# A graph attention layer and a routed feed-forward layer on one core: plain 128-row loads, node sums split between two engines, weight splits moved, the adjacency stream started later

## What is computed

```python
h = inlayer2 @ W.T + b
f1, f2 = h @ w1 + b1, h @ w2 + b2
logits = f1[:, None] + f2[None, :]
bias = -1e9 * (1 - (adj > 0))
x = x + softmax(leaky_relu(logits, 0.01) + bias) @ layernorm(x)
xf = layernorm(x)
probs = softmax(xf @ gate_w + gate_b)          # top 2 of 8 kept: cw
for each expert e:
    acc += cw[:, e] * (gelu(xf @ W1[e] + b1[e]) @ W2[e] + b2[e])
out = x + acc
```

## Time and profile before

| | before |
|---|---|
| median of 3 runs | 521.45 us (521.21 to 522.33) |
| the profiled execution | 521.97 us |
| its span, first to last instruction | 520.4 us |
| mean granted TensorE clock | 0.969 of full speed |
| busy: TensorE, VectorE, ScalarE, GpSimd | 474.6, 437.2, 211.1, 55.1 us |
| moved by DMA | 44.47 MB, read from HBM 92.38 MB |

### The profile page before, as it was taken

How to read it: one execution, slowest core, us unless ns; L and a number is a source line. 1 busy time by engine, 2 the same in 40 slices (tenths; PEclk the granted TensorE clock), 3 DMA queues, 4 the chain that set the end, 5 groups by cost and what they waited for, 6 DMA issues and landing times.

```text
span 520.4 us, 5922 instructions
## 1 busy us (share of the span) xinstructions
PE 474.6 (91%) x1760; PEld 232.5 (45%) x1760; DVE 437.2 (84%) x720; ACT 211.1 (41%) x322; POOL 55.1 (11%) x74
## 2 busy tenths in 40 slices
PE   1997879758999999999999999789999999999996
PEld 1976434413444544444444434334434444444442
DVE  0159379999999999999999998397989898988985
ACT  0127400001011110200102114579898888888884
POOL 5000410990200101010000000000000000000000
PEclk9997979789999999999999999979999999999999
DMA  6999999970393975929500000833443575534410
GB/s 132 195 168 117 213 166 147 92 72 1 26 105 33 89 72 46 105 15 104 52 0 0 0 0 9 148 95 66 116 82 101 97 124 110 116 101 101 120 60 22
DMA packets 36432, 44.47 MB, mean 85 GB/s; under 512 B 2320, under 2 KB 24768, under 8 KB 36416
## 3 DMA queue, kind: packets, MB, share of 16 engines
q0 software_dynamic: 16896, 16.78, 34.9%
q1 hardware_dynamic: 18704, 27.46, 22.0%
q10 hardware_dynamic: 816, 0.03, 0.1%
HBM read 92.38 MB, written 2.23 MB: 182 GB/s over the span
## 4 chain that ended last, share of the span: by engine, by line
PE 65%; DVE 16%; issue 7%; DMA 5%; ACT 4%; another core or an unknown queue 1%; SPq 1%; DVEq 1%; ACTq 0%
PE bank L1007 29%; DVE c L804 7%; PE bank L1045 4%; PE bank L1047 4%; PE bank L1046 4%; PE bank L1034 4%; PE bank L1035 4%; PE bank L1036 4%; DMA share<-in_L_gnn_inlayer 2%; PE bank L953 2%; PE bank L945 2%; PE bank L928 2%; DMA share<-shares 2%; ACT mask L544 2%; DVE xs L691 2%
## 5 line engine op out<-in xcount | busy, mean ns | idle before, releaser
L1007 PE MATMUL bank<-c,Y 128*128 128x512 f32 x512 | 234.9, 610 | 18.8 <-DVE c L804 18.7
L804 DVE SCALAR_TENSOR_TENSOR c<-g_row,r_col,maskT 128x512 f32<-128x512 uint8 (+1 forms) x256 | 196.1, 806 | 14.7 <-PE bank L1007 10.7
L1007 PEld LDWEIGHTS bank<-c,Y 128*128 128x128 f32 x512 | 94.5, 193 | 140.9 <-issue 81.5
L847 DVE TENSOR_TENSOR mask<-mask,share 128x1024 f32<-128x1024 f32 x64 | 78.3, 1223 | 23.1 <-ACT mask L544 16.1
L544 ACT ACTIVATE mask<-bank,b1T 128x512 f32<-128x512 f32 x128 | 83.8, 688 | 24.0 <-PE bank L1036 22.4
L853 DVE TENSOR_TENSOR maskT<-mask,maskT 128x1024 f16<-128x1024 f32 x64 | 78.3, 1224 | 0.0
L551 ACT ACTIVATE maskT<-mask 128x1024 f16<-128x1024 f32 x64 | 67.4, 1053 | 4.1 <-DVE mask L847 4.0
L1045 PE MATMUL bank<-maskT,w2h 128*128 128x512 f16 x128 | 49.1, 383 | 6.6 <-DVE maskT L853 6.1
L1035 PE MATMUL bank<-share,w1h 128*128 (+1 forms) x128 | 49.0, 383 | 0.0
L1046 PE MATMUL bank<-maskT,w2h 128*128 128x512 f16 x128 | 49.0, 383 | 0.0
L1047 PE MATMUL bank<-maskT,w2l 128*128 128x512 f16 x128 | 49.0, 383 | 0.0
(11 more groups left out here) (143 smaller groups left out, 343.9 us busy)
## 6 DMA issues: line engine op xcount, KB each, us to landing
mask<-in_adj POOLq DMA_DIRECT2D x32, 512.0 KB, 17.7
share<-shares SPq DMA_DIRECT2D x16, 1024.0 KB, 8.2
share<-in_L_gnn_inlayer SPq DMA_DIRECT2D x8, 256.0 KB, 8.7
share<-in_x SPq DMA_DIRECT2D x8, 256.0 KB, 20.1
out<-c SPq DMA_DIRECT2D x8, 256.0 KB, 3.8
share<-in_L_ffn_W SPq DMA_DIRECT2D x1, 1024.0 KB, 22.0
x<-in_x SPq DMA_DIRECT2D x1, 256.0 KB, 10.1
W_sb<-in_L_gnn_W SPq DMA_DIRECT2D x1, 64.0 KB, 1.9
```

Source lines behind the costliest of these rows:

```text
L804: dve.scalar_tensor_tensor(c[:, k % CR].rearrange("p (s i) -> p s i", i=32), g_row[:, bass.ds(s * ST, ST)].rearrange("p (s i) -> p s i", i ...
L847: dve.tensor_tensor(hw[:, e % 2], h[:, e % 2], wb[:, e].unsqueeze(1).to_broadcast([P, FC, ST]), ALU.mult).then_inc(hw_done, 1)
L1007: mm(bank[:, par, :], Y[:, k], c[:, k % CR], start=(k == 0), stop=(k == NK - 1)).then_inc(c_used, 1)
```

## The change

1. **Loads.** inlayer2 and x come in two DMAs each, over all 128 partitions with rows of 8 KB: node j = 32p + k on partition p, chunk k. To match, a turn reads its 32 words of a block with a step of 8 words (32 bytes) instead of side by side.
2. **Hold.** POOL waits for both halves of inlayer2 before load 0, and for both halves of x before load 1.
3. **f split.** For chunks KP = 20 to 31 VectorE makes f1 and f2 from inlayer2 itself (two products and two sums over 12 x 128 elements), TensorE keeps chunks 0 to 19. For this the vectors G = W.T w come as rows on all partitions as well. All eight copies into in2T are ScalarE's now.
4. **f1 rows and g_row by parts.** Only part 0 is made ahead; the other seven f1 rows stand in supertile 0 behind k = 3, 7, ..., 27 on TensorE, and ScalarE makes their part of g_row there. The f1 rows read in2T with a step of 128 words.
5. **Row sums.** 16 of them stay ahead of supertile 0, the other 16 go behind its products k = 0 to 15; the step on all_rows moves from k = 4 to k = 22 (S_PRE + 6).
6. **x2, W1, W2.** x2 comes in one DMA, still behind the last f1 row. W1 and W2 wait in addition for the end of supertile 0.
7. **Weight halves.** ScalarE makes the high halves in supertile 1 (behind W1 and W2), VectorE the low halves in supertile 2, eight operations of 512 elements. GpSimd keeps the gate's and b2's.
8. The prologue's order on VectorE: the products and sums, all statistics, then the maxima. Supertiles 1 and 2 are written out ahead of the loop on ScalarE and VectorE.

```diff
             dve.wait_ge(gc_done, 1)
-            dve.tensor_copy(G12[:], bank[:, 4, 0:4]).then_inc(g_copied, 1)
-            for b in range(0, NB, 2):
-                dve.wait_ge(in2t_ready, b + 1)
-                dve.tensor_copy(in2T[:, ST * b:ST * b + ST], bank[:, TURN[b % 4], :]).then_inc(in2t_dve, 1)
+            dve.tensor_copy(G, bank[:, 4, 0:2 * D].rearrange("p (v d) -> p v d", v=2)).then_inc(g_copied, 1)
+            dve.tensor_copy(G12[:], bank[:, 4, 2 * D:2 * D + 4]).then_inc(g_copied, 1)
+            dve.wait_ge(g_copied, 2)
+            dve.wait_ge(in2_in[1], 16)
+            dve.tensor_tensor(prod[:, 0:NK - KP], in2_j[:, KP:NK], G[:, 0:1].to_broadcast([P, NK - KP, D]), ALU.mult)
...
+            dve.tensor_reduce(f1_col[:, KP:NK], prod[:, 0:NK - KP], AX_X, ALU.add)
...
-            mask32 = mask[:].rearrange("p r s j -> p r (s j)").bitcast(U32)
+            mask32 = mask[:].rearrange("p r s j -> p r (s j)").bitcast(U32).rearrange("p r (s w b) -> p r s b w", s=PS_, w=32)
...
-                dve.transpose(at32v[:, par, PS_ * p:PS_ * p + PS_, :].rearrange("p s w -> p (s w)"),
+                dve.transpose(at32v[:, par, PS_ * p:PS_ * p + PS_, :].rearrange("p s (b w) -> p s b w", b=NB),
                               mask32[:, par * NP + p]).then_inc(turned, 1)
...
-                    if first and k == 4:
+                    if first and k == S_PRE + 6:
                         dve.wait_ge(S_ready, 1)
...
+                    if isinstance(s, int) and s == 2 and k % 3 == 0 and k < 24:
+                        v, cols = k // 12, slice(k // 3 % 4 * 512, k // 3 % 4 * 512 + 512)
...
+                        dve.wait_ge(whi_made, v + 1)
+                        ins = dve.scalar_tensor_tensor(lo, raw, W_SCALE, hi, ALU.mult, ALU.subtract)
```

SyncE and POOL:

```diff
-            for b in (0, half):
-                for q in range(Q):
-                    sp.dma_start(dst_k(in2_j, q)[:, b:b + half],
-                                 by_chunk(in2)[q].rearrange("a b e d -> a b (e d)")[:, b:b + half]).then_inc(in2_in[b // half], 16)
+            for n in range(2):
+                part = slice(n * half, (n + 1) * half)
+                sp.dma_start(in2_j[:, part], by_k(in2)[:, part]).then_inc(in2_in[n], 16)
...
             sp.wait_ge(f1row_ready, NB)
-            sp.dma_start(x2[:, 0:TS], x_rows[:, 0:TS]).then_inc(xn_in[0], 16)
-            sp.dma_start(x2[:, TS:NK], x_rows[:, TS:NK]).then_inc(xn_in[1], 16)
+            sp.dma_start(x2[:], x.rearrange("(n p) d -> p n d", p=P)).then_inc(xn_in, 16)
+            sp.wait_ge(c_used, NK)
             sp.wait_ge(y_rows, NK + 1)
             sp.wait_ge(S_ready, 1)
...
+            for n in range(2):
+                pool.wait_ge(in2_in[n], 16)
             load_adj(0, 0)
+            for n in range(2):
+                pool.wait_ge(xj_in[n], 16)
             load_adj(1, 1)
...
             load_adj(3, 1)
-            split(w1raw, w1h[:], w1l[:], arrived=(w_in, 32))
-            split(w2raw, w2h[:], w2l[:])
```

ScalarE and TensorE:

```diff
+                        if p + 1 < NB:
+                            g_part(p + 1)
...
+                    if p == 6 and isinstance(s, int) and s == 1:
+                        act.wait_ge(w_in, 32)
+                        for raw, hi in ((w1raw, w1h[:]), (w2raw, w2h[:])):
+                            act.activation(hi, raw, ACT.Copy, scale=W_SCALE).then_inc(whi_made, 1)
...
+            in2T_i = in2T.rearrange("d (k p) -> d p k", p=P)
+
+            def f1_row(b):
                 need(pe, grow_ready, b - len(ROWS) + 1)
-                mm(bank[:, ROWS[b % len(ROWS)], :], G12[:, 0:1].to_broadcast([P, P]), in2T[:, ST * b:ST * b + ST],
+                mm(bank[:, ROWS[b % len(ROWS)], :], G12[:, 0:1].to_broadcast([P, P]), in2T_i[:, ST // NK * b:ST // NK * b + ST // NK, :],
                    start=True, stop=True).then_inc(f1row_ready, 1)
...
+                    if first and k < NK - S_PRE:
+                        ins = row_sum(S_PRE + k)
+                        if S_PRE + k == NK - 1:
+                            ins.then_inc(S_ready, 1)
+                    if first and k % 4 == 3 and k // 4 + 1 < NB:
+                        f1_row(k // 4 + 1)
```

More of the change, by code:

```diff
@@ L181, in gnn_moe_kernel @@
         xj_in = [sem(f"xj_in{i}") for i in range(2)]
-        xn_in = [sem(f"xn_in{i}") for i in range(2)]
+        xn_in = sem("xn_in")
         w_in = sem("w_in")
@@ L391, in _, with split @@
             splits = [0]
-            def split(raw, hi, lo, arrived=None):
-                if arrived is not None:
-                    pool.wait_ge(*arrived)
+            def split(raw, hi, lo, done):
                 n, splits[0] = splits[0], splits[0] + 1
@@ L443, in _ @@
                 act.dma_start(dst, src).then_inc(small_in if n < 1 else late_in, 16)
-            for b in range(1, NB, 2):
+            act.wait_ge(dve_const, 1)
+            for b in range(NB):
                 act.wait_ge(in2t_ready, b + 1)
                 act.activation(in2T[:, ST * b:ST * b + ST], bank[:, TURN[b % 4], :], ACT.Copy).then_inc(in2t_act, 1)
[L448 to L454, removed]
-                act.activation(g_nat[:, b], bank[:, ROWS[b % len(ROWS)], :].rearrange("p (e q a) -> p q a e", e=4, q=Q),
-                               ACT.Exp, bias=bias_g[:], scale=STEEP).then_inc(grow_ready, 1)
             act.wait_ge(b1_ready, 1)
@@ L623, in stats @@
                 return ins
-            dve.wait_ge(xj_in[0], 64)
-            stats(0, B1)
+            for n in range(2):
+                dve.wait_ge(xj_in[n], 16)
+                last = stats(n * B1, (n + 1) * B1)
+            link(last)
+            for k in range(NK):
+                ins = dve.bn_aggr(mv1[:, k], st1[:, k])
+            ins.then_inc(mv1_ready, 1)
             dve.wait_ge(fcol_made, 1)
-            f12 = bank[:, 4, 2 * P:2 * P + 2 * NK].rearrange("p (k v) -> p v k", v=2)
-            dve.tensor_copy(f1_col[:], f12[:, 0])
-            dve.tensor_copy(f2_col[:], f12[:, 1])
-            link(dve.tensor_scalar(nf2[:], f12[:, 1], -1.0, None, ALU.mult))
+            f12 = bank[:, 4, 2 * D + 32:2 * D + 32 + 2 * KP].rearrange("p (k v) -> p v k", v=2)
+            dve.tensor_copy(f1_col[:, 0:KP], f12[:, 0])
+            link(dve.tensor_copy(f2_col[:, 0:KP], f12[:, 1]))
+            link(dve.tensor_scalar(nf2[:], f2_col[:], -1.0, None, ALU.mult))
             dve.tensor_reduce(part_max[:, 0:1], f1_col[:], AX_X, ALU.max)
@@ L671, in _ @@
                 row_chunk(k)
-            for p in range(2, NP):
+            for p in range(NP):
                 turn(1, p, 0)
@@ L797, in supertile @@
                         dve.wait_ge(turned, (s + 1) * NP)
-                    if first and k == 0:
-                        dve.wait_ge(grow_ready, NB)
+                    if k == 0:
+                        dve.wait_ge(grow_ready, 1 if first else NB)
                     need(dve, c_used, s * NK + k - CR + 1)
@@ L835, in _ @@
             supertile(0, 0, 1, first=True)
-            with dve.Fori(0, NS // 2 - 1) as i:
+            supertile(1, 1, 2)
+            supertile(2, 0, 2)
+            with dve.Fori(1, NS // 2 - 1) as i:
                 supertile(i * 2 + 1, 1, i + 2)
@@ L913, in _ @@
             pe.wait_ge(brep_done, 1)
-            mm(bank[:, 4, 0:2], W_sb[:], w_col[:], start=True, stop=True)
-            mm(bank[:, 4, 2:4], b_rep, w_col[:], start=True, stop=True).then_inc(gc_done, 1)
+            for v in range(2):
+                mm(bank[:, 4, D * v:D * v + D], w_rep[:, v], W_sb[:], start=True, stop=True)
+            mm(bank[:, 4, 2 * D:2 * D + 2], W_sb[:], w_col[:], start=True, stop=True)
+            mm(bank[:, 4, 2 * D + 2:2 * D + 4], b_rep, w_col[:], start=True, stop=True).then_inc(gc_done, 1)
             pe.wait_ge(pool_const, 1)
             def turn_in2(b):
-                pe.wait_ge(in2_in[b // (NB // 2)], 64)
-                need(pe, in2t_act if b % 2 else in2t_dve, (b - 2) // 2)
+                pe.wait_ge(in2_in[b // (NB // 2)], 16)
+                need(pe, in2t_act, b - 3)
                 for e in range(4):
@@ L950, in _ @@
             for n in range(2):
-                pe.wait_ge(xj_in[n], 64)
-            for k in range(NK):
-                ins = mm(bank[:, 3, P:P + D], rs1[:, k:k + 1].to_broadcast([P, P]), x_j[:, k],
-                         start=(k == 0), stop=(k == NK - 1))
-            ins.then_inc(S_ready, 1)
+                pe.wait_ge(xj_in[n], 16)
+            for k in range(S_PRE):
+                row_sum(k)
             def post_a(s):
```

97 lines of the change are left out of this document (56 added, 41 removed).

## The result

| | before | after |
|---|---|---|
| median of 4 runs each, same chip | 521.75 us (521.21 to 522.33) | 539.53 us (537.84 to 541.97) |
| the profiled execution, its span | 521.97, 520.4 us | 540.31, 538.7 us |
| ratio after to before | | 1.0344 [1.03, 1.0389] |

The kernel became slower by 17.8 us. The forecast was 531.0 (+9.3), its range 515 to 541: right in sign and inside the range, but at its upper end, with half of the loss missed.

What follows compares the result with a forecast made beforehand. The front was taken as bound by bytes. Terms of -0.1 us to supertile 0's copy, +4.4 at supertile 1's and +5.0 in supertile 2 made +9.4, a forecast of 531.0 us, range 515 to 541 without the doubled turns.

Steps and rivals of the forecast that it cites:

- Front: Up to load 1's landing: bound by bytes, x2 no longer ahead; load 1 near 60.5 against 66.64 us, -6.1.
- the 14.3 us for inlayer2 and x: Front: time for their 4.2 MB at 293 GB/s, ahead of the end of load 1.
- The adjacency's 40 us: Front: time counted for the two adjacency loads, 0 and 1.
- rival 3: The hold does nothing: load 0 starts so late that load 1 lands at 64; 3.5 us later, 535; 5%.
- Supertile 0: Five f1 rows (4.3 us) and eight row sums (1.7) behind load 1 add +6.0; copy at 91.1.
- Load 2: Issued behind the step on all_rows at 81.5, lands at 114.3 us; VectorE waits 18 us in supertile 1.
- its lone 24: Load 2: an adjacency load alone takes 24 us from first issue, with tail and landing.
- Rival 1: Load 2 is hardly slowed and lands below about 105 us; total near 519 (514 to 522); 18%.
- Supertile 1: Copy at 114.3 + 26.6 + 1.5 = 142.4 against 137.96, +4.4: splits of 15.4 us go, a wait of 18 comes.
- Supertile 2: VectorE's low halves take 5.5 us, part of it in idle time: +5.0 (4.5 to 5.5).
- Stepped reads: Turns reading words 32 bytes apart on VectorE cost nothing in the sum; f1 rows, if doubled, 1 to 3 us.
- Rival 2: The turns double, up to 2.4 us each, 27.5 us more; total 558; decided by turns over 1.3 us; 15%.

Runs made afterwards that it cites:

- experiment 8: Kernel before with weight halves moved off GpSimd, x2 held until load 1 has landed, W1 and W2 until load 2 has: 502.19 us, ratio 0.9635.
- experiment 5: Changed kernel without GpSimd's four waits for inlayer2 and x: 539.09 us, ratio 1.0332.
- experiment 6: Changed kernel with f1 rows read in runs of 16 words and ScalarE putting the row in order: 538.31 us, ratio 1.0333.
- Experiment 4: Changed kernel with load 2 issued before GpSimd waits for the step on all_rows: 528.15 us, ratio 1.0139.
- experiment 1: Changed kernel with each turn reading its words side by side again (mask in another order): 522.42 us, ratio 1.0019.
- experiment 2: Kernel before with only the turns' read stepped by 32 bytes (mask in another order): 539.87 us, ratio 1.0364.
- experiment 3: Changed kernel with the four turns of a load stepping 1, 2, 4 and 8 words: 531.92 us, measured once.
- experiment 9: Changed kernel with inlayer2 and x loads in old order, turns side by side, load 2 issued early, f1 rows in runs of 32 words: 514.94 us, ratio 0.9868.
- experiment 7: Kernel before with only W1 and W2 splits moved off GpSimd to ScalarE (high) and VectorE (low halves): 508.82 us, ratio 0.9762.

## Why the prediction was right in sign, by luck, and short in size

- **Front: right, undersized.** Load 1 at 58.03 for 60.5. The term that was too high is the 14.3 us for inlayer2 and x, by 293 GB/s; the new loads run at 421. The adjacency's 40 us held (17.81, where x had landed, to 58.03 is 40.2), and x2's place behind load 1, counted at 7.2 us, is worth 6.0 (experiment 8). The hold has no part in it (experiment 5), as the name of rival 3 says; its price of 3.5 us was wrong too.
- **Supertile 0: right by two errors.** Copy forecast at 91.1, seen at 92.07. Load 1 came 2.5 earlier and the rest ran some 1.4 shorter than I had it (there was hardly a restart: TensorE idled 0.62 us at load 1), against that f1 rows took 4.1 more (experiment 6), which I had put at nothing in the sum and at 1 to 3 in the margin, and a turn 0.8.
- **Load 2: the mechanism right.** Issue forecast at 81.5, seen at 79.28; landing 114.3, seen 109.09; wait 18, seen 12.84. From issue to landing 29.8 us for 32.8: 5.8 over its lone 24, where I had added some 9 for x2 and the weights. Experiment 4 shows the cause, the issue behind the step on all_rows. Rival 1 asked for a landing under 105 and fell.
- **Supertile 1: right by size of its parts.** 142.4 forecast; 5.2 off for the landing, 1.85 off for the stretch from turn to copy (26.25 in experiment 1, for 26.6 + 1.5: the low clock around the restart cost nothing that shows, and VectorE is busy for 4.89 us of 110 to 115 there), 2.9 on for the stepped turns: 138.3, and 138.28 is seen.
- **Supertile 2: low halves 3.8 for 5.0.** VectorE's idle time took up more of them than I allowed. With 3.1 for the turns that makes the 6.95.
- **Stepped reads: the step that failed.** "Each turn reads words 32 bytes apart, at no cost in my sum". It costs 0.78 us a turn, 2.6 us in each supertile from 3 to 6, 17 to 19 us in all (experiments 1 and 2). I took the price from rows that are not like it: a stepped read of PSUM and a copy of 32 elements. None streams SBUF through VectorE, and the prediction said so and still took zero. Rival 2 had the mechanism and its point of decision (over 1.3 us) right and the size too high, 2.02 for 2.4 us and 27.5 us for some 17. The forecast's other terms were too high by some 8 us between them (+9.4 for the 1 us of experiment 1), and that is why the total stayed in the range: luck, not foresight. The sign is luck too. What the sum did count nets to 0.2% in experiment 1, next to nothing; that the kernel is clearly slower comes from the term that the sum had at zero.

By its parts, then: the moved splits are worth -12.8, the wait for load 2 some +11.4, the stepped f1 rows some +1.2 while that wait is there, the stepped turns +17 to +19, the hold nothing beside the new loads. Load 1's 8.6 us (6.0 for x2's place, 2.6 for the loads' form) are used up by the row sums, the f1 rows and a stepped turn in supertile 0, whose copy comes 0.8 later.

## What to carry to other kernels

When a DMA's layout is made simpler and a compute instruction has to step through it instead, count that instruction first: here the form of the loads brought 2.6 us once, and the read cost 0.78 us in each of 32 turns. With two 4-byte words of every 16 bytes the turns here cost nothing extra (experiment 3). A load issued behind a wait in a program's written order inherits every delay of what that wait is for, so a step that is put off is to be followed into the queue that stands behind it.

## What the runs showed that I had not expected

- A 32x32-block transpose of 128x1024 words on VectorE takes 1.23 us with a step of one or two words and 2.02 with four or eight: 0.78 us, not a doubling.
- TensorE's float32 product with 512 moving columns goes from 0.86 to 1.70 us when the columns are read 512 bytes apart in SBUF, while ScalarE's read of PSUM with a step costs nothing (684 ns either way).
- inlayer2 and x in DMAs over 128 partitions with rows of 8 KB ran at 421 GB/s between 7 and 16 us; in DMAs to 32 partitions with rows of 2 KB, also held ahead of the adjacency, at 221 (experiment 9). Which of the two, the partitions or the length of a row, makes the difference was not tried.
- SyncE's issue of W1 took 9.27 us in the changed kernel and 1.49 in the kernel before, both for a 1 MB transfer beside a running adjacency load. Its cause was not tried.
- The granted clock around an idle stretch of TensorE: 0.57 over the 8 us that hold the end of one of 6.52 us, 1.00 over those that hold one of 2.60 (experiments 7 and 8, VectorE's waits there being 6.92 and 2.89). In the changed kernel it was 0.50 in 105 to 110 us, while TensorE stood idle for 11.33 us until 111.78, and 0.71 in 115 to 120; it cost nothing that shows.
